# Cross-attention on one core: the low parts of the contexts made by VectorE in one instruction instead of by GpSimd in two

## The reference, cut to what matters

```python
# x: (16, 100, 128), ctx: (16, 1444, 128), H = 16 heads of 64
q = (x @ Wq + bq).reshape(b, ql, H, 64)
k = (ctx @ Wk + bk).reshape(b, kl, H, 64)
v = (ctx @ Wv + bv).reshape(b, kl, H, 64)
attn = softmax(einsum('bqhd,bkhd->bhqk', q, k) / 8)
out = einsum('bhqk,bkhd->bqhd', attn, v).reshape(b, ql, 1024) @ Wo + bo
y = x + out
return (y - mean(y)) * rsqrt(var(y) + 1e-5) * gamma + beta
```

## Time and profile before

| | us |
|---|---|
| median of 3 runs | 888.51 (886.20 to 889.07) |
| the profiled execution | 887.55 |
| its span in the profile | 885.7 |
| TensorE busy | 857.1 (97%) |
| VectorE busy | 802.3 (91%) |
| ScalarE busy | 757.1 (85%) |
| GpSimd busy | 477.1 (54%) |

### The profile page before, as it was taken

How to read it: one execution, slowest core, us unless ns; L and a number is a source line. 1 busy time by engine, 2 the same in 40 slices (tenths; PEclk the granted TensorE clock), 3 DMA queues, 4 the chain that set the end, 5 groups by cost and what they waited for, 6 DMA issues and landing times.

```text
span 885.7 us, 19608 instructions
## 1 busy us (share of the span) xinstructions
PE 857.1 (97%) x7328; PEld 614.5 (69%) x7328; DVE 802.3 (91%) x996; ACT 757.1 (85%) x1061; POOL 477.1 (54%) x517
## 2 busy tenths in 40 slices
PE   7799989999999999999999999999999999999996
PEld 6466766677777677776767677777767767767675
DVE  4798899999899999989999998999999899999984
ACT  3798978888989888898988889898888989888983
POOL 3143597976637374565728556373844657276210
PEclk9999999999999999999999999999999999999999
DMA  8598988999999999999999999999999999999995
GB/s 239 116 186 196 198 156 170 196 227 199 229 209 216 210 205 232 216 205 213 221 214 223 210 208 216 215 216 210 219 220 214 202 227 210 192 194 221 213 177 125
DMA packets 683041, 180.79 MB, mean 204 GB/s; under 512 B 654596, under 2 KB 682052, under 8 KB 682948
## 3 DMA queue, kind: packets, MB, share of 16 engines
q1 hardware_dynamic: 681332, 178.48, 102.1%
q10 hardware_dynamic: 1344, 0.53, 0.2%
q0 software_dynamic: 272, 0.53, 0.2%
HBM read 15.35 MB, written 0.82 MB: 18 GB/s over the span
## 4 chain that ended last, share of the span: by engine, by line
DVE 36%; PE 27%; ACT 16%; issue 13%; DMA 4%; SPq 3%; ACTq 0%; DVEq 0%; POOLq 0%; POOL 0%
DVE p_lo L920 16%; DVE nmax L905 15%; PE ps L662 12%; PE ps L623 11%; ACT p L1064 8%; ACT p_hi L1072 3%; DMA pt_hi<-p_hi 3%; DVE rsum L911 2%; ACT unused L1029 2%; PE ps L478 1%; DVE rinv L913 1%; SPq L422 1%; ACT c_hi L1013 1%; SPq L413 1%; ACT o_t L1087 1%
## 5 line engine op out<-in xcount | busy, mean ns | idle before, releaser
L920 DVE SCALAR_TENSOR_TENSOR p_lo<-p,rinv,p_hi 128x1444 f16<-128x1444 f32 x200 | 368.6, 1843 | 2.5 <-ACT p_hi L1072 2.1
L1072 ACT ACTIVATE p_hi<-p,rinv 128x1444 f16<-128x1444 f32 x200 | 299.8, 1499 | 52.2 <-DVE rinv L913 51.0
L905 DVE TENSOR_REDUCE nmax<-ps 128x1 f32<-128x1446 f32 x200 | 329.9, 1650 | 12.3 <-PE ps L623 11.8
L1064 ACT ACTIVATE p<-ps,nmax 128x1446 f32<-128x1446 f32 x200 | 291.8, 1459 | 30.1 <-DVE nmax L905 28.1
L662 PE MATMUL ps<-pt_hi,c_hi 128*128 128x256 f16 (+1 forms) x1232 | 253.0, 261 | 6.3 <-DMA pt_hi<-p_hi 4.0
L662 PE MATMUL ps<-pt_hi,c_lo 128*128 128x256 f16 (+1 forms) x1232 | 253.0, 261 | 0.0
L623 PE MATMUL ps<-ct_hi,g_hi 128*128 128x482 f16 (+3 forms) x624 | 155.9, 368 | 4.8 <-ACT p L1064 2.4
L623 PE MATMUL ps<-ct_hi,g_lo 128*128 128x482 f16 (+3 forms) x624 | 155.6, 367 | 0.0
L623 PE MATMUL ps<-ct_lo,g_hi 128*128 128x482 f16 (+3 forms) x624 | 155.6, 367 | 0.0
L662 PEld LDWEIGHTS ps<-pt_hi,c_hi 128*128 128x128 f16 x1232 | 114.1, 98 | 44.4 <-issue 10.9
L1179 POOL CAST g_hi<-g_raw 128x400 f16<-128x400 f32 x60 | 32.4, 540 | 202.5 <-DVE g_raw L856 202.5
(11 more groups left out here) (134 smaller groups left out, 790.8 us busy)
## 6 DMA issues: line engine op xcount, KB each, us to landing
c_raw<-in_ctx_dram SPq DMA_DIRECT2D x32, 256.0 KB
pt_hi<-p_hi SPq DMA_TRANSPOSE x200, 3.5
pt_lo<-p_lo SPq DMA_TRANSPOSE x200, 3.7
c_raw<-in_ctx_dram SPq DMA_DIRECT2D x16, 192.0 KB
c_raw<-in_ctx_dram SPq DMA_DIRECT2D x48, 18.0 KB
out_dram<-late_sb SPq DMA_DIRECT2D x16, 50.0 KB
x_sb<-in_x_dram SPq DMA_DIRECT2D x1, 600.0 KB
o_t<-in_L_xattn_Wq_dram SPq DMA_DIRECT2D x2, 256.0 KB, 4.5
```

What stands on the lines that cost most here:

```text
L905: dve.tensor_reduce(nmax[:, n % RING:n % RING + 1], ps[:, bank:bank + 3, 0:KEYW], AX.XY, ALU.max, negate=True).then_inc(s_nm, 1)
L920: dve.scalar_tensor_tensor(out=p_lo[:, n % LOS, 0:KL], in0=p32[:, n % P32S, 0:KL], scalar=rinv[:, i:i + 1], in1=p_hi[:, par, 0:KL], op0=AL ...
L1064: act.activation(p32[:, n % P32S, :].rearrange("p (k w) -> p k w", w=KEYW), ps[:, bank:bank + 3, 0:KEYW], ACT.Exp, bias=nmax[:, i:i + 1], ...
L1072: act.activation(p_hi[:, par, 0:KL], p32[:, n % P32S, 0:KL], ACT.Copy, scale=rinv[:, i:i + 1]).then_inc(s_hi, 1)
```

## The change

GpSimd's `context_lo` is removed with its two instructions per group and its semaphore; its queue now waits for the last group's `s_cl` and copies the tail. VectorE gets a `context_lo` for one group, in the form that line 869 has for batch 0, called after the tile's inverse and its other jobs at r = 5, 7 and 8 (`CLO_AT`), for the contexts of batches 1 to 15: 45 calls. It waits for the group's c_hi and, from batch 2 on, for the same count of results that c_hi waits for and for the tail copy of two batches ago. The buffer `c_scaled` stays under another name for its other users.

```diff
+    CLO_AT = (5, 7, 8)
...
-        c_scaled = sb("c_scaled", [P, TG * D])
+        left_scaled = sb("left_scaled", [P, TG * D])
...
-        s_cs = sem("context_scaled")
...
+            def context_lo(b, g):
+                par, tiles = b % 2, slice(TG * g, TG * g + TG)
+                dve.wait_ge(s_chi, NT * b + g + 1)
+                if b > 1:
+                    dve.wait_ge(s_pv, RESULTS * (b - 1))
+                    dve.wait_ge(s_chl, b - 1)
+                dve.scalar_tensor_tensor(out=c_lo[:, par, tiles, :].rearrange("p t d -> p (t d)"),
+                                         in0=c_raw[:, par, tiles, :].rearrange("p t d -> p (t d)"), scalar=alpha[:, par:par + 1],
+                                         in1=c_hi[:, par, tiles, :].rearrange("p t d -> p (t d)"),
+                                         op0=ALU.mult, op1=ALU.subtract).then_inc(s_cl, 1)
...
+                if r in CLO_AT and w + 1 < B:
+                    context_lo(w + 1, CLO_AT.index(r))
                 if r == (TOP_AT if w else TOP_AT_FIRST) and w + 2 < B:
                     context_scale(w + 2, ps[:, JOB_BANK, :])
...
-            def context_lo(b):
-                par = b % 2
-                pool.wait_ge(s_al, b + 1)
-                for g in range(NT):
-                    tiles = slice(TG * g, TG * g + TG)
-                    if NT * b + g > NT:
-                        pool.wait_ge(s_cl, NT * (b - 1) + g)
-                    pool.tensor_scalar(c_scaled[:, :], c_raw[:, par, tiles, :].rearrange("p t d -> p (t d)"),
-                                       alpha[:, par:par + 1], 1.0, ALU.mult, ALU.mult).then_inc(s_cs, 1)
-                    pool.wait_ge(s_cs, NT * (b - 1) + g + 1)
-                    pool.wait_ge(s_chi, NT * b + g + 1)
-                    pool.tensor_tensor(c_lo[:, par, tiles, :].rearrange("p t d -> p (t d)"), c_scaled[:, :],
-                                       c_hi[:, par, tiles, :].rearrange("p t d -> p (t d)"), ALU.subtract).then_inc(s_cl, 1)
-                pool.wait_ge(s_cl, NT * b)
-                context_tail(b)
...
-                    context_lo(b)
+                    pool.wait_ge(s_cl, NT * b)
+                    context_tail(b)
```

More of the change, by code:

```diff
@@ L1200, in leave_m_lo @@
             def leave_m_lo(g):
-                heads, at = slice(HG * g, HG * g + HG), c_scaled[:, :].rearrange("p (n w) -> p n w", w=P)
+                heads, at = slice(HG * g, HG * g + HG), left_scaled[:, :].rearrange("p (n w) -> p n w", w=P)
                 pool.wait_ge(s_mh, g + 1)
@@ L1241, in leave_lo @@
                 n, w = raw.shape[1], raw.shape[2]
-                at = c_scaled[:, 0:n * w].rearrange("p (n w) -> p n w", w=w)
+                at = left_scaled[:, 0:n * w].rearrange("p (n w) -> p n w", w=w)
                 if i:
```

## The result

The changed kernel takes 893.83 us (median of 8 runs, 891.95 to 897.98), the kernel before takes 887.75 us on the same chip (8 runs, 885.58 to 890.51). The ratio is 1.0069, interval 1.0046 to 1.0092: 6.1 us slower. I had forecast 890.8 us, range 886.5 to 897.5. The time is in the range, and on the side of the rival that I had given 0.23: GpSimd gets in first, 895.6 us.

What follows compares the result with a forecast made beforehand. TensorE and the VectorE-ScalarE loop were taken to run at nearly the same pace; 2.9 us of insertion delay in windows 3 to 14, less about 0.6, gave +2.3: 889.9 us, or 890.8 against the median, range 886.5 to 897.5.

Steps and rivals of the forecast that it cites:

- GpSimd gets in first: Rival: tile 5, even windows; GpSimd's line 1191 holds c_lo, 0.8 us each, 4.8 in all, 895.6 us; chance 0.23.
- likeliest case: VectorE's insertions are partly covered by idle time: +2.3 us, 889.9, or 890.8 against the median; chance 0.50.
- the start of tile 5: Even windows, tile 5: c_lo starts at 378.66, GpSimd's line 1191 at 378.70, 0.04 us deciding who holds whom.
- The forecast's terms: Delay from c_lo at tiles 5, 7, 8: +0.34 us per even window, +0.15 per odd, 2.9 over windows 3 to 14.
- 0.6 taken off: About 0.3 us of row maximum waiting for TensorE and some 0.3 of TensorE's slack, taken off 2.9 us.
- Windows 0 to 2: TensorE there is further ahead or behind for other reasons: cost taken as 0, bounds 0 and +0.7 us.
- Removed work worth 0: GpSimd's 45 multiplications and 45 subtractions, 127.2 us, are off the chain; removing them gains 0 by itself.
- The relief rival: Rival: with less GpSimd work, p_lo loses 6.6 us of its excess on the path, 884.2 us; chance 0.10.
- TensorE hides it: Rival: TensorE's slack recovers each window's delay before the next, no change, 888.5 us; chance 0.13.
- Full price: Rival: VectorE is the bound and nothing hides, 36 insertions x 0.70 = 25 us, 914 us; chance 0.04.
- The form's price: Each c_lo instruction on VectorE takes 0.748 us, as line 869's do; the skill's halving rule would give some 910 us.
- The signs: VectorE busy 832 to 838 us, idle before tile 5 and 8 row sums nearly gone, TensorE's waits up about 2 us.

Runs made afterwards that it cites:

- experiment 1: Changed kernel plus one GpSimd wait: its last results subtraction starts only after the next context's first low part; 890.44 us, ratio 1.0032.
- experiment 6: Kernel before, with the low part of context 2 alone (made in window 1) moved to VectorE; 886.71 us, ratio 0.9987.
- experiment 3: Changed kernel with no low parts made for contexts 1 to 15; tail copy and transpose follow c_hi; 885.12 us, ratio 0.9975.
- experiment 5: Kernel of experiment 1 plus one spare VectorE instruction of c_lo's form at tile 9 of windows 0 to 14; 898.57 us, ratio 1.0122.
- experiment 7: Kernel of experiment 6 with GpSimd's bias addition in four back-to-back pieces, VectorE waiting only for its batch's piece; 888.03 us, ratio 1.0006.
- experiment 8: Kernel before with GpSimd's bias addition in four back-to-back pieces, VectorE waiting only for its batch's piece; 888.26 us, ratio 1.0007.
- experiment 4: Changed kernel with GpSimd still making its removed multiplication and subtraction, into a buffer nobody reads; 904.01 us, ratio 1.0185.
- experiment 9: Changed kernel without c_lo's two redundant waits (results, and tail copy of two batches ago); 889.33 us, ratio 1.0028.
- experiment 10: Kernel of experiment 7 with each of the four bias addition pieces waiting for the one before; 883.45 us, ratio 0.9964.
- experiment 11: Kernel of experiment 8 with each of the four bias addition pieces waiting for the one before; 888.02 us, ratio 1.0011.

## Why the prediction was wrong in its likeliest case and right in its rival

**The step that failed** is the one on the start of tile 5: I took c_lo to begin at 378.66, GpSimd's line 1191 at 378.70, and gave the likeliest case to the one that starts first. Both starts were right. After, they are 379.56 and 379.61, again 0.04 apart, but a lead of that size loses. That both are released by the end of the same p_lo fits the lead's being the same to 3 ns in all six even windows (0.042 to 0.045 us). It was one race, run six times. A lead of 0.04 us, read from rows with two decimals, should have made the two cases equal at least.

**The rival's price** was right: 0.8 us per even window, 4.8 in all. Measured: 0.82 in window 6, and in windows 3 to 14 together 627.48 - 623.25 = 4.2. By medians it is 3.4. Its sum was +7.1, measured +6.1.

**The forecast's terms**, in the kernel without the collision (experiment 1): even window +0.34, measured +0.32 in window 6; odd +0.15, measured -0.13 in window 7 (53.54 against 53.68) and +0.05 in window 11 (53.55 against 53.50): nearly nothing. With 0.6 taken off I had +2.3 in windows 3 to 14. The sums say +1.7, but before's holds a single long window (54.66 us, window 13); by the windows that repeat it is 5 x 0.32, 0.72 in window 14, and 6 x -0.05 to +0.05 for the odd ones: 2.0 to 2.6. The size was right within what one trace can tell. That 0.6 comes off was an estimate that no run tested.

**Windows 0 to 2** I took as 0, with +0.7 as the bound. Window 0 costs +1.3, outside the bound; experiment 6 shows that it belongs to the insertions there. What covers less than I assumed in window 0 I have not tried out. Window 1 gives 0.9 back and window 2 takes 0.3.

**Removed work worth 0** was wrong in window 1: 2.65 us there (experiments 3 and 6). GpSimd's low parts stood in its queue ahead of the long bias addition, and I had looked at who waits for them, not at when the addition behind them starts. Without them it starts earlier against p_lo, which then takes 3.61 us instead of 6.26. With c_lo on VectorE the tail copy waits for that, and only 0.97 of it is left (5.30), the 0.9 that window 1 gives back. So the forecast's +2.3 was met (+2.8) by two larger terms, -2.2 and +5.1, of which I had one at 0 and the other at half: the agreement of the total is in part luck. The relief rival had the quantity, p_lo's excess: p_lo's sum went from 368.6 to 363.8 us, 4.8 less where I had given 6.6, but of that I can place only the 0.97 in window 1.

**TensorE hides it** falls: experiment 5 shows +0.71 per window of either kind. **Full price** falls for the three tiles of the change, where idle time does cover part, and holds at tile 9, where there is none.

**The form's price.** Median 0.752, least 0.741 us, against 0.748 by the earlier trace rows. The halving for two SBUF sources that are not bf16 (the Trainium skill, Vector Engine (DVE) Microarchitecture Reference, "Points that are easy to get wrong") did not show in any of the 45 (1.03 ns per element between 512 and 1444 elements); by that rule the kernel would have taken some 910 us, and the measured time was 894.

**The lock.** p_lo at 6.26 us beside a 4.51 us addition, c_lo at 1.54 beside a 0.95 us subtraction, and GpSimd's subtraction at 1.46 when it loses show that one engine waits while the other works. The Trainium skill (SBUF — State Buffer, "SBUF: two separate sides") calls it an exclusive lock: the one that starts first gets the pair for its whole instruction. The trace agrees that one of the two blocks, but it differs twice: with 0.04 us of lead the one that starts first by its row lost, and over a row of instructions the lock was kept across all of them (experiments 7 and 8). Even a lead of 0.20 us lost before the bias addition: p_lo starts at 124.78, the addition at 124.98, and the copy ahead of it was still running (GpSimd, kernel before):

```profile
124.73 0.29 POOL L1215 COPY c_tail<-c_hi 72x128 f16<-72x128 f16 x1
```

**The signs.** VectorE busy: 832 to 838 forecast, 830.0 measured, just outside. c_lo instructions of 1.3 to 1.6 us at tile 5 of even windows were named as the mark of GpSimd first, and they are there at 1.53. The idle times before the row sum are gone (0.49, 0.33 and 0.75 us in window 6, now none at these tiles), and TensorE's wait for transposed p_hi grew from 1.8 to 4.6 us; its wait for ScalarE's o_t, which was not among the listed ones between 240 and 700 us, is 5.8.

## What to carry to other kernels

Where two engines share a port, look in the timeline for the two starts that come out closest, and price both outcomes: a race settled by 0.04 us repeats identically in every pass of a loop. A fixed order (a wait on the cheap side, one tile's shift, or a redundant wait fewer) is worth what the whole race is. And a removed instruction of a half idle engine can still have been worth something: look at which long instruction stands behind it in the queue and what that one holds when it starts earlier or later, in the windows that are not like the rest.

## What the runs showed that I had not expected

- **The lead that wins.** c_lo lost with leads of 0.042 to 0.047 us and won with 0.048 (window 4 of experiment 4), 0.072 to 0.075 (experiment 9) and 0.16 us (odd windows). In these cases GpSimd's subtraction waits for its own cast before it; against the bias addition, which follows a copy without such a wait, leads of 0.20 (before) and 0.22 us (experiment 8) lost. Leads of 0.047 and 0.048 us are 1 ns apart in the rows, so where the border lies, or whether it is one of start times at all, is open.
- **Back to back instructions count as one.** p_lo took 6.26 us beside one addition of 100x2048, 5.81 and 6.69 beside four of 100x512 without waits, and 2.73 and 3.00 with a wait between them. The price was on GpSimd's side: the four took 6.62 us (experiment 10) and 8.17 (experiment 11) in place of 4.95.
- **A satisfied wait costs.** Without two waits that were long met, c_lo took 0.732 us instead of 0.752 (experiment 9), and led GpSimd's subtraction by 0.03 us more.
